# A Perceiver block on one core: values as weights in column halves, probabilities divided before they are turned, three head pairs in flight

## The reference

```python
q, k = l2norm(q) * qs, l2norm(k) * ksc
q, k = rotary_xpos(q, k)
sim = einsum('bhwid,bhwjd->bhwij', bq * 8, bk)     # bk, bv: the block before and its own
sim = where(mask, -max, sim)                       # causal, and at most 128 back
attn = softmax(sim, axis=-1)
out = einsum('bhwij,bhwjd->bhwid', attn, bv)
x = x + out.transpose(...).reshape(b, n, 512) @ wo
# then a layer norm, h @ w1 + b1, a * gelu(g), @ w2 + b2, added to x
```

## Time and profile before

| | before |
|---|---|
| three runs, us | 1074.54, 1073.37, 1075.62 |
| median, us | 1074.54 |
| profiled execution, first to last instruction (its own time is not listed apart) | 1071.0 |
| mean granted TensorE clock | 0.989 |
| busy PE / PEld / DVE / ACT / POOL, us | 1017.7 / 944.8 / 822.1 / 663.1 / 205.3 |
| instructions PE / DVE / ACT / POOL | 8678 / 3031 / 1542 / 265 |
| DMA moved | 21.71 MB |

### The profile page before, as it was taken

How to read it: one execution, slowest core, us unless ns; L and a number is a source line. 1 busy time by engine, 2 the same in 40 slices (tenths; PEclk the granted TensorE clock), 3 DMA queues, 4 the chain that set the end, 5 groups by cost and what they waited for, 6 DMA issues and landing times. The chain is left out here.

```text
span 1071.0 us, 25673 instructions
## 1 busy us (share of the span) xinstructions
PE 1017.7 (95%) x8678; PEld 944.8 (88%) x8679; DVE 822.1 (77%) x3031; ACT 663.1 (62%) x1542; POOL 205.3 (19%) x265
## 2 busy tenths in 40 slices
PE   3899999999999999999999999988999999999997
PEld 3789999999999999999999998976879898989897
DVE  5897877777777777777777777578888889889753
ACT  4466565665565665565665566475676777667653
POOL 0111111111111111111111111350006203164213
PEclk9999999999999999999999998998999999999999
DMA  6000000000000000000000100420001000010000
GB/s 202 23 3 12 11 1 0 11 4 10 13 2 0 11 3 11 13 2 0 11 3 11 34 2 1 155 47 1 2 6 55 2 2 21 21 60 2 2 21 21
DMA packets 29073, 21.71 MB, mean 20 GB/s; under 512 B 13269, under 2 KB 26537, under 8 KB 28969
## 3 DMA queue, kind: packets, MB, share of 16 engines
q1 hardware_dynamic: 27985, 20.21, 6.3%
q10 hardware_dynamic: 984, 0.13, 0.1%
HBM read 19.23 MB, written 1.05 MB: 19 GB/s over the span
## 5 line engine op out<-in xcount | busy, mean ns | idle before, releaser
L295 PEld LDWEIGHTS pv_ps<-v,pt 128*128 128x128 f32 x1792 | 216.0, 193 | 8.8 <-issue 2.4
L295 PE MATMUL pv_ps<-v,pt 128*128 128x65 f32 x1792 | 216.4, 273 | 2.7 <-DVE o L820 1.4
L798 DVE CUSTOM_DVE_ANT_0 s_sb<-s_ps,pen,mstate 128x256 f32<-128x256 f32 (+1 forms) x512 | 199.9, 447 | 13.3 <-issue 10.4
L493 ACT ACTIVATE probs<-s_sb,mbias 128x256 f32<-128x256 f32 (+1 forms) x512 | 203.1, 469 | 0.0
L660 POOL TENSOR_TENSOR o<-o,alpha 128x260 f32<-128x260 f32 x128 | 86.2, 673 | 572.6 <-ACT alpha L487 572.6
L502 ACT ACTIVATE pt<-turn 128x512 f32<-128x512 f32 x128 | 76.2, 595 | 121.3 <-PE turn L282 107.4
L282 PE MATMUL turn<-ident,probs 128*128 128x128 f32 x896 | 124.3, 279 | 4.1 <-DVE ql L776 3.2
L282 PEld LDWEIGHTS turn<-ident,probs 128*128 128x128 f32 x896 | 99.1, 145 | 14.2 <-DVE ql L776 3.4
L820 DVE TENSOR_TENSOR o<-o,pv_ps 128x260 f32<-128x260 f32 x128 | 54.0, 422 | 46.9 <-PE pv_ps L295 36.1
L271 PE MATMUL s_ps<-kh,qh 64*128 64x256 f32 (+1 forms) x512 | 79.4, 306 | 4.2 <-DVE kl L770 1.8
L770 DVE TENSOR_TENSOR kl<-proj,kh 128x512 fp32r<-128x512 f32 (+1 forms) x63 | 41.2, 655 | 50.0 <-ACT kh L480 49.7
(11 more groups left out here) (420 smaller groups left out, 2743.9 us busy)
## 6 DMA issues: line engine op xcount, KB each, us to landing
raw<-in_ctx SPq DMA_DIRECT2D x24, 128.0 KB, 2.1
f_wqkv_raw<-in_L_ffn_wqkv SPq DMA_DIRECT2D x6, 512.0 KB, 5.3
wkv_raw<-in_L_xattn_Wkv SPq DMA_DIRECT2D x2, 1024.0 KB, 8.4
f_w_raw<-in_L_ffn_w SPq DMA_DIRECT2D x8, 256.0 KB, 5.0
f_w_raw<-in_L_ffn_w SPq DMA_DIRECT2D x2, 640.0 KB
wq_raw<-in_L_xattn_Wq SPq DMA_DIRECT2D x1, 1024.0 KB, 8.8
wout_raw<-in_L_xattn_Wout SPq DMA_DIRECT2D x1, 1024.0 KB, 10.2
f_wo_raw<-in_L_ffn_wo SPq DMA_DIRECT2D x2, 512.0 KB, 4.5
```

What stands on the lines that cost most here:

```text
L295: last = pe.matmul(t.pv_ps[:, u, :], t.pt[g % 2][:, u, kt, :], t.v[:, kt, h, :], start=(kt == 0), stop=(kt == kts - 1))
L493: last = act.activation(t.probs[g % 2][:, u, 0:kts * P], t.s_sb[g % 2][:, u, 0:kts * P], ACT.Exp, bias=t.mbias[:, at:at + 1], scale=0.125)
L798: last = dve.tensor_tensor_reduce(out=t.s_sb[g % 2][:, u, 0:width], in0=t.s_ps[g % 2][:, u, 0:width], in1=t.pen[:, 0:width], scale=1.0, sc ...
```

## The change

The values become the weights. `weighted_values` loads the 64 value columns of a head as weights, and the turned probabilities move: for each block of keys and each head one product, of 256 columns for the first block (both blocks of queries) and of 128 for the second. The output is 64 partitions of the bank: head 0 in the lower half of the columns of the array, head 1 in the upper, so a pair fills 128 partitions and comes out turned already. `turn_output` and `t.o` go; two pairs fill the bank, and `output_hi` and `output_lo` split it from there, twice per unit.

The sums no longer come from a column of ones. `exponentials` take them as accumulators, and a new step on VectorE, `divided`, takes the reciprocal and multiplies the probabilities in place, four products per pair, before `turn_probs`. `t.p` has six tiles, so three pairs are in flight, and `maxima` waits for the transposes of three pairs back.

In the loops, `divided` of pairs 0 and 1 stands behind the maxima of pairs 1 and 2, that of pairs 2 and 3 in the next iteration, behind the first `heads_lo` and the second `add_down`. `turn_probs(T-1, 0, 0)` moves behind the scores of pair 2, `exponentials(T, 1, 1)` from the start of an iteration to before the gelus of the iteration before. Behind the loop `up(LAST-1, 2)` moves ahead of `project_output`. The second layer's weight pieces are split in the order of the first layer's; SP loads `w11` before `w12`; GpSimd's loop is written anew, with `add_constants` ahead of the hidden columns of its unit and the splits of `w10`, `w11`, `w12` and `w2` spread between those of unit 4.

```diff
-SPLIT_ORDER = [(name, 0) for name in PIECES] + [(name, 1) for name in ("wqkv0", "wqkv1", "wqkv2", "wo", "w12", "w10", "w11", "w2")]
+SPLIT_ORDER = [(name, l) for l in range(DEPTH) for name in PIECES]
...
             def turn_probs(u, p, o):
-                pe.wait_ge(s["p_ready"], 2 * at + o + 1)
+                pe.wait_ge(s["p_scaled"], 2 * at + o + 1)
...
             def weighted_values(u, p):
-                if at:
-                    pe.wait_ge(s["o_ready"], at)
-                for o in range(2):
-                    pe.wait_ge(s[("pt_act", "pt_dve")[o]], at + 1)
-                    v = [t.v[:, (2 * u + k) % 4, 2 * p + o, :] for k in range(2)]
-                    pe.matmul(t.pv[:, 0, o, :], t.pt[o][:, 0, :], v[0], start=True, stop=True)
-                    pe.matmul(t.pv[:, 1, o, :], t.pt[o][:, 1, :], v[0], start=True, stop=False)
-                    last = pe.matmul(t.pv[:, 1, o, :], t.pt[o][:, 2, :], v[1], start=False, stop=True)
+                if p % 2 == 0 and at:
+                    pe.wait_ge(s["ot_lo"], 2 * u + p // 2)
+                cols = p % 2 * L
+                pe.wait_ge(s["pt_act"], at + 1)
+                pe.wait_ge(s["pt_dve"], at + 1)
+                for kt in range(2):
+                    for o, rows in enumerate((slice(0, LDH), slice(LDH, P))):
+                        out = t.pv_bank[rows, cols + kt * P:cols + L]
+                        moving = t.pt[o][:, 2 * kt:2 + kt, :].rearrange("p k q -> p (k q)")
+                        last = pe.matmul(out, t.v[:, (2 * u + kt) % 4, 2 * p + o, :], moving, start=(kt == 0), stop=(kt == 1))
                 last.then_inc(s["pv_done"], 1)
-            def turn_output(u, q, bank):
...
             def exponentials(u, p, o):
...
+                                          accum_out=of_pair(t.p_sums, u, p)[:, q, o:o + 1])
...
-            def output_hi(u, q, bank):
-                act.wait_ge(s["o_turned"], count(2, u, q))
+            def output_hi(u, half):
+                act.wait_ge(s["pv_done"], count(PAIRS_OF, u, 2 * half + 1))
...
             def maxima(u, p):
-                if at >= 2:
-                    dve.wait_ge(s["t_done_even"], at - 1)
+                if at >= 3:
+                    dve.wait_ge(s["t_done_even"], at - 2)
...
-            def normalise(u, p):
...
+            def divided(u, p):
+                dve.wait_ge(s["p_ready"], 2 * count(PAIRS_OF, u, p))
+                dve.reciprocal(of_pair(t.p_inv, u, p), of_pair(t.p_sums, u, p)).then_inc(s["inv_ready"], 1)
+                dve.wait_ge(s["inv_ready"], count(PAIRS_OF, u, p))
+                for o in range(2):
+                    for q, cols, _ in keys_of:
+                        last = dve.tensor_scalar(p_tile(u, p, o)[:, cols], p_tile(u, p, o)[:, cols], of_pair(t.p_inv, u, p)[:, q, o:o + 1], None,
+                                                 ALU.mult)
+                    last.then_inc(s["p_scaled"], 1)
...
                 if valid(T - 1):
-                    normalise(T - 1, 0)
                     store_turned(T - 1, 1)
...
                     heads_lo(T, 0, 0, t.g[0])
+                if valid(T - 1):
+                    divided(T - 1, 2)
...
-                    normalise(T - 1, 1)
+                    output_lo(T - 1, 0)
                 if valid(T - 3):
                     add_down(T - 3, 1, t.g[0])
+                if valid(T - 1):
+                    divided(T - 1, 3)
...
-                    normalise(T - 1, 2)
...
-                    normalise(T - 1, 3)
...
-                    output_lo(T - 1, 0, t.g[2])
+                    output_lo(T - 1, 1)
                 if valid(T):
                     maxima(T, 1)
+                    divided(T, 0)
...
-                    output_lo(T - 1, 1, t.g[1])
...
                     maxima(T, 2)
+                    divided(T, 1)
...
+            for T in range(0, UNITS + 2):
+                if valid(T - 3):
+                    hidden_lo(T - 3, 5)
...
+                if valid(T - 2):
+                    add_constants(T - 2)
...
+                if valid(T - 2):
+                    hidden_lo(T - 2, 0)
+                    hidden_lo(T - 2, 1)
+                if T == 6:
+                    split_second("w12")
+                if valid(T - 2):
+                    hidden_lo(T - 2, 2)
+                    hidden_lo(T - 2, 3)
...
+            t.p = sb("p", [P, 6, 3 * P])
```

More of the change, by code:

```diff
@@ L1143, in valid, with p_tile, of_pair, both_pairs @@
         return 0 <= u < UNITS
-    def turned_outputs(u, q):
-        if u == LAST and q:
-            return [x[:, 0:4 * P].rearrange("p (k n) -> p k n", k=4) for x in t.xt]
-        return [o[:] for o in t.ot]
+    def p_tile(u, p, o):
+        return t.p[:, (2 * (PAIRS_OF * u + p) + o) % 6, :]
+    def of_pair(buffer, u, p):
+        return buffer[:, (PAIRS_OF * u + p) % 3]
+    def both_pairs(o, half):
+        return o[:, 2 * half:2 * half + 2, :].rearrange("p k n -> p (k n)")
     def y_value(u, q):
@@ L1203, in _ @@
                     second_layer("w10", "up_done", 20)
-                if T == 2:
+                    second_layer("w11", "up_done", 22)
                     second_layer("w12", "up_done", 24)
@@ L1215, in _ @@
                     second_layer("wo", "e_done", 8)
-                if T == 3:
-                    second_layer("w11", "up_done", 22)
             rows = out.rearrange("b (t p) d -> p (b t) d", p=P)
@@ L1278, in _ @@
             for part in t.xt:
-                pool.memset(part[:].bitcast(F32), 0.0)
-            pool.memset(t.v[:, :, :, LDH:LDH + 1], 1.0).then_inc(s["constants_set"], 1)
+                last = pool.memset(part[:].bitcast(F32), 0.0)
+            last.then_inc(s["constants_set"], 1)
             for piece in weight_pieces(t, args, 0):
@@ L1604, in _ @@
                     scores(T - 1, 2)
+                    turn_probs(T - 1, 0, 0)
                     turn_probs(T - 1, 0, 1)
@@ L2106, in store_turned, with output_lo @@
                 dve.tensor_copy(t.pt[1][:].rearrange("p k q -> p (k q)"), t.turn[1][:, 0:3 * P]).then_inc(s["pt_dve"], 1)
[L2108 to L2121 removed]
+            def divided(u, p):
[7 more added lines that the diff above has]
+                    last.then_inc(s["p_scaled"], 1)
+            def output_lo(u, half):
+                dve.wait_ge(s["ot_hi"], count(2, u, half))
+                hi, lo = (both_pairs(o, half) for o in t.ot)
+                low_part(lo, t.pv_bank[:], hi).then_inc(s["ot_lo"], 1)
             def add_output(u, q, bank):
@@ L2394, in _ @@
                     maxima(T, 2)
-            output_lo(LAST, 1, t.s[0])
+                    divided(T, 1)
             gate(LAST - 1, 1, t.g[1])
```

154 lines of the change are left out of this document (46 added, 108 removed).

## The result

The changed kernel takes **1104.0 us** (median of 4 runs, 1102.3 to 1105.6) against 1074.3 of the kernel before on the same chip: a ratio of 1.028, with a 95% interval of 1.026 to 1.030. It is slower by 29.7 us; the forecast was slower by 21.7, and 1104 lies in the range. The profiled spans are 1103.6 and 1071.0 us, so 32.6 us are to be explained.

A forecast was written before the change was run, and what follows sets the result against it. TensorE (95% busy) bounds the kernel, VectorE close behind and pacing it after the change. Full iterations 13.2, start 6, last 1.5 and tail 1 add 21.7 us, giving 1096 us; range 1082 to 1108, eight in ten 1066 to 1110.

The forecast's parts named there:

- three waits of TensorE that I named: Sign of being right: TensorE idle before turn_probs(2), before the projection behind the heads and before project_output(1).
- The division: On VectorE, per pair: a reciprocal of 0.2 us and four products starting 0.25 and 0.32 apart, 1.34 us.
- normalise: VectorE step removed per pair: reciprocal and product, put at 0.55 us from its start to the next instruction.
- Section B: VectorE from add_output(T-2, 1) to the last heads_lo, where TensorE waits for heads and x: +2.4 us.
- Section A: VectorE from the gates to the next add_output: +1.5 us, all before gate(T-3, 3), less 0.6 of slack.
- The sum: Four full iterations at 3.3, 13.2; three at the start, 6; the last, +1.5; behind the loop, +1: +21.7 us.
- The last iteration and the tail: Last iteration: 2.4 from VectorE less TensorE's 0.9, +1.5; behind the loop, division, normalise, turned outputs and delay: +1 us.
- TensorE's gain: TensorE saves 1.9 us a unit (0.1 to 2.7) on turn_output and weighted_values; none reaches a full iteration's end.
- TensorE stays the bound: Rival: TensorE remains the bound, faster by 1.9 us times 8 units, 15, so 1060 us; chance 0.21.
- GpSimd's hold: Rival: GpSimd stalls VectorE's added products; one hit a unit, 8 us more, 1104; two, 1112; chance 0.14.
- Column halves in turn: Rival: weighted_values' column halves don't run side by side; TensorE gains 0.1 a unit, not 1.9; 1097 us; chance 0.03.
- Costed at nothing: GpSimd's new order, SP's loads, the third buffer pair: nothing; ScalarE's added sums, 3.0 us, hidden by its waits.

The follow-up runs named there:

- no_division: The changed kernel with the division of the probabilities left out (no reciprocal, no products; turn_probs waits for the exponentials alone): 1062.2 us, ratio 0.990.
- old_gpsimd: The changed kernel with GpSimd's and SP's order of the kernel before the change: 1110.3 us, ratio 1.036.
- late_3: The changed kernel with divided(3) moved behind heads_lo(1) and the next unit's cosine product before the first gate: 1101.7 us, ratio 1.027.

## Why the prediction was right, and where it was not

**What held.** The sign, the place and the chain: VectorE's order sets the pace, TensorE waits before turn_probs(2), and what it saved went into waiting. The no_division run shows that the division is the cause. VectorE waits for the first gelu 3.01 us, no shorter than before (2.20, in the fence below). Of the three waits of TensorE that I named, only the first came in full; those before the projection behind the heads and before project_output(1) are 0.6 and 0.4 us in the whole stage, and in their place TensorE waited 5.9 us for add_output(0) and 4.3 before turn_heads for the normed rows (f_wide).

**The division**, forecast at 1.34 us a pair, took 1.24 in the free burst. **normalise** was taken at 0.55 from start to start. VectorE's busy time grew by 1.7 us in the free iteration, by 2.4 without the rows that GpSimd held, not the 3.2 of the steps; the 39 us forecast also started from the 35.8 of the earlier trace rows, while the iteration itself had 34.3.

**Section B**, forecast +2.4: from add_output to the heads_lo of 888.40 it is 18.7 us, against 16.6, +2.1. Right. **Section A**, forecast +1.5 less 0.6 of slack: from that heads_lo to add_output it takes 24.06 us, and took 24.05. VectorE's rows of before in this section, its first gate and the rotation of the next unit, and GpSimd's constants:

```profile
877.84 0.48 DVE L2194 SCALAR_TENSOR_TENSOR f_hidden<-f_g,f_b,f_gelu 128x256 f32<-128x256 f32 x1 [2.20 <-ACT f_gelu L1833]
...
887.00 1.65 DVE L2067 TENSOR_TENSOR f_rot<-f_rot,f_sin_part 128x1024 f32<-128x1024 f32 x1
888.68 1.66 DVE L2074 TENSOR_TENSOR f_rot<-f_rot,f_k_inv 128x512 f32<-128x512 f32 x1
```

```profile
887.53 2.27 POOL L1251 TENSOR_TENSOR raw<-raw,f_b 128x512 f32<-128x512 f32 x1
```

and gate(T-3, 3) after the change:

```profile
910.00 0.47 DVE L2167 SCALAR_TENSOR_TENSOR f_hidden<-f_g,f_b,f_gelu 128x256 f32<-128x256 f32 x1
```

The first gate came no earlier: 4.87 us behind that heads_lo, and 4.86 before. From it to gate(T-3, 3) it took 16.73 us, and 16.46 before: the added products are there, but before the change two rows of this stretch took 1.65 and 1.66 us in place of 1.23 and 0.69, while GpSimd ended a hidden_lo and added the constants, and the new order has the constants elsewhere. With GpSimd's old order (old_gpsimd) the stretch takes 17.84 us (+1.4, forecast +1.5), section A 1.1 us more than before the change, and the iteration 43.8, where I had 43.9. So the step that failed is a term that I put at nothing, GpSimd's new order: it gave back 1 us of the 3.3. The free iteration lost 2.2.

**The sum.** I had 13.2 for four full iterations; they lost 15.9 (4.9, 2.2, 3.3 and 5.5). What they lost beyond 2.2 each is in the main the granted clock, which the prediction did not look at: 3.4 us at half in the first and the third and 6.8 in the fourth, up to 1.7, 1.7 and 3.4 us lost. GpSimd's hold on VectorE grew in the first alone (7.4 us, 5.1 before; in the fourth 6.0, and 6.1 before). The start, forecast 6, lost 8.3, with 10.2 us more at half clock than before. The last iteration and the tail were the largest miss: 2.5 forecast, 8.5 measured up to add_output(7, 1). There I let TensorE keep its saving because VectorE is free; but the waits before turn_probs (2.31 us at 1051.54) and before weighted_values (1.89 at 1010.81) came, and 10.2 us at half clock with them. Behind the last add_output nothing was lost: 31.2 us against 31.3, where I had 1. That the time still lies in the range is in part luck: the clock, at nothing in the sum, took up to 17.1 us, and GpSimd's order gave some 6 back. The range's lower end does not follow from what I named for it: half of the terms of the iterations gives about 1086, not 1082.

**TensorE's gain**, 1.9 a unit, measured 2.2 by the account. The weighted values were mis-sized: 0.80 us a pair, under my lower end of 0.83. The two heads' column halves run wholly side by side. The Trainium skill (TensorEngine Tiling (Array Packing), Key Properties) says that different tiles load and multiply in parallel; by that rule I had 0.83, and the row agrees.

**The rivals.** *TensorE stays the bound* fell; even without any division the time is 1062, so its 1060 was as good as out of reach. *GpSimd's hold* named the measured time, 1104, but that is chance: its 8 us of hits came (9.7 on the new products, 5.8 net by VectorE's rows), while the 21.7 on which it put them left out the clock. *Column halves in turn* fell.

**Costed at nothing.** GpSimd's new order was worth 6 us to this kernel. The sums that ScalarE adds were not tried alone; in the iteration without division it is busy 31.4 us against 30.1, and TensorE waits 5.0 us for it in all.

What stays open: pair 3 alone, the third pair of buffers, which was not taken away again, and how much of the clock's fall comes from the long wait and how much from the short gaps around it, since late_3 had fewer of these and lost no less.

## What to carry to other kernels

Before you move work from TensorE to another engine, look at where TensorE will stand when the moved work has to be done: a pair whose product was wanted at once cost 15 us, pairs that are turned 5 to 9 us behind their exponentials 8.5 each, and moving the work to engines with more free time made it worse here, since what TensorE waited for came later. Price a new wait of TensorE with the clock behind it: here 33.2 us of waits came with up to 17 more. Look at what a third engine does beside the work that you add: the same additions of constants cost 1 us more an iteration in one place than in another. And leave the new step out first: the time without it (1% faster) is about the most that another order of it alone can reach.

## What was not expected of the hardware

- The granted clock falls behind waits as short as 1.7 us while TensorE is busy again. In the changed kernel each of the eight stretches at half clock after 735 us begins within a wait of 1.8 us or more, or at most 1.3 us behind one. But not each wait is followed by one: that of 1.66 us at 877.05 was not, nor those of 2.35 at 830.29 and at 997.73, while that of 1.66 at 875.40 in late_3 was. So between 1.7 and 2.4 us the length of the wait alone does not decide it in these traces.
- Float32 products with 64 columns of weights, one per half of the array, pair up: the four products of a head pair (eight rows), of 256 and 128 moving columns, take 0.80 us, where six of 65 columns (twelve rows) took 1.28.
- The four products of a pair take 1.05 us on VectorE; on ScalarE they took rows of 0.48 and 0.59 us each, and as two products on GpSimd 0.61 to 1.60 us each.
